# One step count per engine as semaphore, and a planner that charges for tiling changes and second waits

## The reference

```python
x = L0(x, cond, ctx)   # adaln; attention 16 heads x 64 with rotary embedding; gelu
x = L1(x, cond, ctx)   # 16 heads x 8 ("small"); gelu (tanh form)
x = L2(x, cond, ctx)   # 16 heads x 64 without rotation ("flat"); gated gelu
x = L3(x, cond, ctx)   # 16 heads x 8, q and k normalised per head; gates; gated silu
# every attention:
h = ln(x) * (1 + scale) + shift
a = softmax(q(h) @ k(source).T * dh ** -0.5)
x = (a @ v(source)) @ wo + bo + x
```

## Time and profile before

| | us |
|---|---|
| median of 3 runs (lowest, highest) | 1694.85 (1692.47, 1695.61) |
| the profiled execution's own time | 1697.18 |
| its span, first to last instruction | 1695.4 |
| TensorE busy (matmuls) | 1523.6 |
| weight loads | 1202.8 |
| VectorE | 1402.9 |
| ScalarE | 1094.9 |
| GpSimd | 911.8 |

### The profile page before, as it was taken

The page is one execution under the profiler, slowest core; times in us unless marked ns, Lnnn a source line. Parts: engine busy times, 40 slices in busy tenths (PEclk is TensorE's granted clock), DMA queues, the critical chain, the costliest instruction groups (busy, mean ns, idle before and its releaser), DMA issues.

```text
span 1695.4 us, 41504 instructions
## 1 busy us (share of the span) xinstructions
PE 1523.6 (90%) x15228; PEld 1202.8 (71%) x15228; DVE 1402.9 (83%) x3745; ACT 1094.9 (65%) x4765; POOL 911.8 (54%) x1028
## 2 busy tenths in 40 slices
PE   6988999899989899999998989999988999989865
PEld 5876777677768677776777777767766778767643
DVE  5878788988997778898897868998898878888864
ACT  1766778657575777757477667766666686775632
POOL 3746454655664546555665645545565654554432
PEclk9999999999999999999999999999999999999985
DMA  9100000000000000000000000000000000000000
GB/s 325 38 2 1 2 2 2 7 6 3 7 7 2 1 2 2 6 3 7 6 4 7 2 1 2 2 7 2 7 7 7 2 2 1 2 2 3 3 0 4
DMA packets 14441, 20.96 MB, mean 12 GB/s; under 512 B 4064, under 2 KB 10784, under 8 KB 14240
## 3 DMA queue, kind: packets, MB, share of 16 engines
q1 hardware_dynamic: 14240, 18.31, 3.3%
HBM read 17.25 MB, written 1.05 MB: 11 GB/s over the span
## 4 chain that ended last, share of the span: by engine, by line
PE 46%; DVE 36%; POOL 7%; ACT 6%; issue 3%; DMA 0%; SPq 0%; POOLq 0%; DVEq 0%; ACTq 0%
DVE negmax L1025 9%; PE ps L688 9%; PE ps L720 6%; PE ps L571 6%; PE ps L731 5%; ACT E L776 5%; POOL E L879 4%; DVE E L1125 4%; PE ps L703 3%; DVE xn L986 3%; PE ps L651 3%; DVE E L1077 2%; PE ps L665 2%; PE ps L588 2%; PE ps L740 2%
## 5 line engine op out<-in xcount | busy, mean ns | idle before, releaser
L776 ACT ACTIVATE E<-ps,negmax 128x128 f32<-128x128 f32 x2048 | 719.4, 411 | 264.2 <-DVE negmax L1025 263.5
L879 POOL TENSOR_TENSOR E<-E,rinv 128x512 f32<-128x512 f32 x512 | 525.3, 1042 | 382.3 <-DVE rinv L1033 380.6
L776 ACT ACTIVATION_READ_ACCUMULATOR E<-ps,negmax 128x1 f32 x2048 | 512.2, 251 | 0.0
L1025 DVE TENSOR_REDUCE negmax<-ps 128x4 f32<-128x512 f32 x512 | 330.2, 681 | 57.9 <-PE ps L651 33.6
L688 PE MATMUL ps<-consts,E 128*128 128x128 f32 x2048 | 318.9, 287 | 40.0 <-POOL E L879 25.7
L1125 DVE COPY E<-ps 128x512 f32<-128x512 f32 x448 | 300.5, 678 | 59.9 <-PE ps L688 57.6
L688 PEld LDWEIGHTS ps<-consts,E 128*128 128x128 f32 x2048 | 235.6, 146 | 115.6 <-issue 66.7
L872 POOL TENSOR_TENSOR E<-E,prod 128x512 f32<-128x512 f32 x128 | 162.4, 1274 | 74.7 <-DVE prod L1080 74.5
L831 POOL TENSOR_TENSOR rstd<-ve,consts 128x1 f32<-128x1 f32 (+1 forms) x192 | 107.9, 563 | 83.4 <-DVE ve L979 82.9
L720 PE MATMUL ps<-E,VV 128*64 128x128 f32 x2048 | 141.6, 285 | 3.2 <-DVE E L1125 2.6
L785 ACT ACTIVATE VV<-ps 128x512 f32<-128x512 f32 x128 | 77.2, 671 | 90.4 <-PE ps L588 90.3
(11 more groups left out here) (130 smaller groups left out, 2755.3 us busy)
## 6 DMA issues: line engine op xcount, KB each, us to landing
w_f<-res_f SPq DMA_DIRECT2D x6, 256.0 KB, 11.8
qT<-in_x SPq DMA_DIRECT2D x16, 64.0 KB, 1.7
w_wq<-res_wq SPq DMA_DIRECT2D x2, 512.0 KB, 7.8
w_wk<-res_wk SPq DMA_DIRECT2D x2, 512.0 KB, 8.4
w_wv<-res_wv SPq DMA_DIRECT2D x2, 512.0 KB, 9.0
w_wo<-res_wo SPq DMA_DIRECT2D x2, 512.0 KB, 9.8
w_cq<-res_cq SPq DMA_DIRECT2D x2, 512.0 KB, 10.9
w_co<-res_co SPq DMA_DIRECT2D x2, 512.0 KB, 13.8
```

Source lines behind the costliest of these rows:

```text
L776: last = nc.scalar.activation(E[p][:, h, :], bank(u, j * N, (j + 1) * N), ACT.Exp, bias=negmax[p][:, h:h + 1], accum_out=sums[p][:, h:h + 1])
L879: tt(e, e, rinv[p][:, T4 * g:T4 * g + T4].unsqueeze(2).broadcast_to([N, T4, N]), ALU.mult).then_inc(signal["prob"], 1)
L1025: nc.vector.tensor_reduce(negmax[p][:, T4 * g:T4 * g + T4], bank(u).rearrange("p (h m) -> p h m", h=T4), AX, ALU.max, negate=True).then_in ...
```

## The change

Three things change. First, the semaphores: each engine has one, which the last instruction of every step raises by one; a wait is for the step's number in that engine's order. Waits for earlier steps of the same engine are left out by the same rule (`fresh`). Second, on TensorE the wait for banks comes after that for the inputs, and several waits of one kind are sorted with the highest number first. An S step raises once, after its last matmul, instead of once per bank; MX0 to MX2 and PJ0 raise too. Where VectorE needs a result of its own from within a step, it uses `vector_part`. Third, the planner: costs of TensorE's steps without the change of tiling, 0.12 for a step whose tiling differs from the one before, 0.1 for each engine beyond the first that must be waited for, banks chosen with that charge, and rope's VectorE steps held until GpSimd has released the older `prod` tile.

```diff
+RETILE = 0.12
+WAIT = 0.1
-    add(PE, "T", 0.14, (DVE, "norm"), fills=("T",))
+    add(PE, "T", 0.13, (DVE, "norm"), fills=("T",))
...
-            add(PE, "S0", 2.1, ...                      # rope
+            add(PE, "S0", 1.95, ...
-            add(PE, f"S{2 * i}", 1.09, ...              # flat
+            add(PE, f"S{2 * i}", 0.99, ...
-        add(PE, "S0", 1.15, ...                         # small
+        add(PE, "S0", 0.95, ...
-        add(PE, f"PT{g}", 0.46, ...
+        add(PE, f"PT{g}", 0.44, ...
-            add(PE, f"MX{g}", 0.45, ...
+            add(PE, f"MX{g}", 0.24, ...
-        add(PE, f"O{i}", 1.1, ...
+        add(PE, f"O{i}", 0.88, ...
...
+def tiling_of(key):
+    _, step, b, _ = key
+    if step[0] == "S":
+        return "rows of 64" if KIND[b] == "flat" else "rows of 32"
+    return "columns of 32" if step[:2] == "MX" else "columns of 64" if step[0] == "O" else None
+
+def turns_heads(key):
+    return key[0] == DVE and KIND[key[2]] == "rope" and key[1] in ("Q0", "Q1", "K0", "K1")
...
-    vacant = {i: 0.0 for i in range(BANKS)}
+    vacant = {i: (0.0, DVE, 0) for i in range(BANKS)}
...
-            start, banks = max(free[e], known[key]), []
-            if fills[key]:
+            start, banks, extra, met = max(free[e], known[key]), [], 0.0, {}
+            if turns_heads(key) and len(roped) > 1:
+                _, old, old_b, old_s = roped[-2]
+                added = (POOL, "R" + old, old_b, old_s)
+                if added not in end:
+                    continue
+                start = max(start, end[added] + REACH[POOL])
+            if e == PE:
+                for a in after[key]:
+                    if a[0] != PE and number[a] > seen[a[0]]:
+                        met[a[0]] = max(met.get(a[0], 0), number[a])
                 n = len(fills[key])
                 open_ = [i for i in vacant if vacant[i] is not None]
-                if len(open_) < n or fills[key][0] not in OWN and len(open_) - n < SPARE:
+                if n and (len(open_) < n or fills[key][0] not in OWN and len(open_) - n < SPARE):
                     continue
-                banks = sorted(open_, key=lambda i: (vacant[i], i))[:n]
-                start = max(start, vacant[banks[-1]])
-            score = (start, AGE * key[3] - way[key], key)
+                covered = lambda i: vacant[i][2] <= max(seen[vacant[i][1]], met.get(vacant[i][1], 0))
+                banks = sorted(open_, key=lambda i: (max(vacant[i][0], start) + (0 if covered(i) else WAIT), i))[:n]
+                for i in banks:
+                    start = max(start, vacant[i][0])
+                    if not covered(i):
+                        met[vacant[i][1]] = vacant[i][2]
+                extra = WAIT * max(len(met) - 1, 0)
+                if tiling_of(key) != tiling:
+                    extra += RETILE
+            score = (start + extra, AGE * key[3] - way[key], key)
...
+DONE = {_key: _i + 1 for _engine in ORDER for _i, _key in enumerate(ORDER[_engine])}
...
-        bank_full = [sem(f"bank_full{b}") for b in range(BANKS)]
-        bank_drained = [sem(f"bank_drained{b}") for b in range(BANKS)]
+        done = {PE: sem("tensor_done"), DVE: sem("vector_done"), ACTE: sem("scalar_done"), POOL: sem("gpsimd_done")}
+        vector_part = sem("vector_part")
-        signal = {n: sem(n + "_ready") for n in sorted(_total)}
...
-                for unit in units:
-                    if vacant(unit):
-                        if fresh(pe, bank_drained[unit[0]], vacant(unit)):
-                            pe.wait_ge(bank_drained[unit[0]], vacant(unit))
+                def vacated():
+                    for by, count in latest_first(*[EMPTY[n, turn - 1] for n, turn in units if turn]):
+                        if fresh(pe, done[by], count):
+                            pe.wait_ge(done[by], count)
...
                     for r, unit in enumerate(units):
                         q0 = 32 * r
-                        mm(bank(unit), qT[p][q0:q0 + 32, 0, :], kT[p][q0:q0 + 32, 0:T4, :], start=True, stop=True)\
-                            .then_inc(bank_full[unit[0]], 1)
+                        last = mm(bank(unit), qT[p][q0:q0 + 32, 0, :], kT[p][q0:q0 + 32, 0:T4, :], start=True, stop=True)
+                    last.then_inc(done[PE], 1)
...
                 elif step[:2] == "PT":
                     g = int(step[2])
-                    count = AT["prob", f"prob{g}", b, s]
-                    if fresh(pe, signal["prob"], count):
-                        pe.wait_ge(signal["prob"], count)
+                    count = DONE[POOL, f"prob{g}", b, s]
+                    if fresh(pe, done[POOL], count):
+                        pe.wait_ge(done[POOL], count)
+                    vacated()
```

More of the change, by code:

```diff
@@ L218, in schedule @@
     free = {e: 0.0 for e in order}
-    vacant = {i: 0.0 for i in range(BANKS)}
-    end, bank_of, table = {}, {}, "exp"
+    vacant = {i: (0.0, DVE, 0) for i in range(BANKS)}
+    end, number, bank_of, table, tiling = {}, {}, {}, "exp", None
+    seen = {e: 0 for e in order}
     left = {key: len(after[key]) for key in cost}
     ready = [key for key in cost if not left[key]]
-    known = {}
+    known, roped = {}, []
     while ready:
@@ L245, in schedule @@
         table = table_of(key) or table
-        if e == PE and start > free[e] + 0.02:
-            start += REFILL
+        if e == PE:
+            if start > free[e] + 0.02:
+                start += REFILL
+            start += extra
+            seen.update(met)
+            tiling = tiling_of(key)
         end[key] = free[e] = start + cost[key] + (TABLE_LOAD if switch else 0)
         order[e].append(key)
+        number[key] = len(order[e])
         ready.remove(key)
+        if turns_heads(key):
+            roped.append(key)
         for unit, i in zip(fills[key], banks):
@@ L274 @@
         _turns[_bank] += 1
[L275 to L310, removed]
+DONE = {_key: _i + 1 for _engine in ORDER for _i, _key in enumerate(ORDER[_engine])}
+FULL, EMPTY = {}, {}
+for _b, _s, _n in UNIT:
+    _last = {"PV": "MX3", "PJ": "PJ" if KIND[_b] == "small" else "PJ1"}.get(_n)
+    _fill = next(_key for _key in ORDER[PE] if _key[2:] == (_b, _s) and (_key[1] == _last or _n in FILLS[_key] and not _last))
+    FULL[UNIT[_b, _s, _n]] = DONE[_fill]
+for _s in range(S):
+    for _b in range(LAST + 1):
+        for _key, _, _, _, _n in steps_of(_b, _s):
+            if _n:
+                EMPTY[UNIT[_b, _s, _n]] = (_key[0], DONE[_key])
+ROPED = [_key for _key in ORDER[DVE] if turns_heads(_key)]
 ROPE_GROUP = {"Q0": 0, "K0": 1, "Q1": 2, "K1": 3}
@@ L484, in _ @@
                 if step == "sum" and b == L3_CROSS and s + STREAMS < S:
-                    count = AT["sum", "sum", b, s]
-                    if fresh(sp, signal["sum"], count):
-                        sp.wait_ge(signal["sum"], count)
+                    count = DONE[DVE, "sum", b, s]
+                    if fresh(sp, done[DVE], count):
+                        sp.wait_ge(done[DVE], count)
                     load(s + STREAMS)
@@ L624, in step_of @@
                     if b == L3_SELF:
[L625 removed]
+                        mm(bank(u, 0, D), hT[p][:, :], c("spread"), start=True, stop=True).then_inc(done[PE], 1)
                     else:
@@ L1063, in step_of @@
+                    tt(gates[p], bank(u, 0, 3 * D), row("g0", 3), ALU.add).then_inc(done[DVE], 1)
                 elif step in ("Q0", "Q1", "K0", "K1") and k == "rope":
```

561 lines of the change are left out of this document (281 added, 280 removed).

## The result

The change made the kernel slower: 1756.84 us (1752.2 to 1760.1) against 1693.67, ratio 1.0365 with a 95% interval of 1.0349 to 1.0381. The forecast was 1668. The mechanism of rival D is the right one: putting the S steps last cost 76 us in the pair of kernels that differ in it alone, where I had 45, and without that cost the kernel was 15 us faster than before, not 27.

What follows compares the result with a forecast made beforehand. TensorE was taken as the nearest bound (busy 1523.6 of 1695.4 us, 46% of the chain, VectorE 36%). Terms -24 -2 +1 -2 = -27 us gave 1668 from the median 1694.85; range 1630 to 1706.

Steps and rivals of the forecast that it cites:

- rival D: Softmax chains starve as S steps come late by one full-size step, 0.89 us; 45 us lost, 1713 us; chance 0.19.
- the change's first part: Fewer changes of tiling on TensorE: 220 of 891 go, 40 us of its time, -24 us at the end (0 to -73).
- the 30 changes of S: Share of S steps in the 220 fewer tiling changes on TensorE, beside 160 for MX and 30 for O.
- rival C: TensorE's order hardly changes, fewer than 80 tiling changes go: 1690 us; sign: TensorE busy above 1510; chance 0.15.
- D's signs: TensorE busy falls, but L688's counterpart's waits for GpSimd, ScalarE's for maxima and VectorE's for TensorE grow by more.
- The number of changes: Changes of tiling in TensorE's static order: from 891 to about 670.
- Their price: One change of tiling between TensorE's weight loads costs 0.17 to 0.20 us; 0.18 taken.
- What it brings at the end: Share of TensorE's saved time that reaches the end: 0.6, between the chain's 46% and nine tenths.
- The semaphores: Half of about 1000 separate waits on TensorE go: -2 us (0 to -7); the S group's one signal: +1.
- The single signal of an S step: One signal for all banks of an S step: 0 to 0.1 us later each, 160 steps, +1 us (0 to +5).
- the 9 us that I worked out from that page: Saving before the release of the maxima from fewer S signals at 0.026 us each; no term rested on it.
- The gate on rope's products: Planner knows VectorE's rope step waits for GpSimd to release a product tile: -2 us, at most -4.

Runs made afterwards that it cites:

- the pair of kernels that differ in it alone: Changed kernel (1756.84 us) against the same with S steps exempt from the tiling charge in the score (1681.1 us), age price 30.
- S exempt: Changed kernel with the 0.12 us tiling charge left out of the score of S steps alone: 1681.1 us, ratio 0.9911.
- the semaphores alone: Changed kernel with the planner of before, so only semaphores and the order of waits are new: 1690.1 us, ratio 0.9970.
- the three pairs with and without the charges: Changed kernel without score charges against charges on all but S, ages 29, 30, 31: 1704.4 and 1725.8, 1697.0 and 1681.1, 1698.3 and 1676.0 us.
- late S in the old kernel: Kernel before with the gate on rope's product tiles and S steps scored 0.12 us later whatever the tiling: 1809.2 us, ratio 1.0666.
- the changed kernel at ages 29 to 31: Changed kernel with 29, 30 (its own) or 31 as the planner's price of a sequence's age: 1779.5, 1756.8, 1768.8 us.
- S alone: Changed kernel where only S steps bear the tiling charge in the score and no other step bears any charge: 1784.2 us, ratio 1.0518.
- the order alone: Kernel before with the planner of the change but the old semaphores: 1764.1 us, ratio 1.0412.
- the old planner with age 29: Kernel before with the gate on rope's product tiles and age price 29 instead of 30: 1760.4 us, ratio 1.0379.

## Why the prediction was wrong

**The failed step** is in the change's first part: "S steps little, since they need four banks and two spare ones", and the 30 changes of S that I counted as a gain. I treated the score as something that sorts equals. It is a strict first key: while any full-size step can start within 0.12 us, a ready S step isn't taken, however long its way. Ten steps in eleven had their inputs there, which I used as the reason why grouping would work; it is the reason why an S step finds such a rival at nearly every turn. The planners of the kernels, run again, count it: an S step that had its banks and could start no later than the step taken was passed over at 1.1 turns on average before, at 6.1 in the changed kernel and at 1.4 with S exempt. The need for six open banks, on which I had built, hardly moved: it turned an S step away at 3.7, 4.0 and 3.3 turns.

**Rival D was mis-sized.** I let an S step be late by one step, 0.89 us. The traces show 4.6 us more for rope, 3.2 for flat, 4.2 for small: over 32, 64 and 64 steps that is 147 + 205 + 269 = 621 us of added delay, where the prediction had 142. Against the kernel with S exempt it is 693 us, and the loss 76, so 0.11 us of time is lost per us of S delay, where I had 0.32. The two errors work against each other: the delay was taken more than four times too small, the share that reaches the end three times too large, so that 45 came as near to 76 as it did by luck. The chance of 0.19 was too low, and the range, up to 1706, ended below the measured time.

**The signs** that the prediction had named misled. TensorE stayed busy for 1516.4 us, which was the sign for rival C (above 1510). Of D's signs, L709's loads wait 67.6 us for GpSimd where L688's waited 15.7, but such entries also moved by the semaphores alone (67.8 in that run). ScalarE's wait for maxima did not grow, it fell from 263.5 to 216.2; what grew is its whole idle time with a releaser, from 590 to 650 us, by the V banks above all, and so did GpSimd's (770 to 830) and VectorE's (268 to 323).

**The number of changes** was forecast at 670 and is 582; of the 154 runs of tiled steps that went, 106 are MX. **Their price** holds: 0.17 to 0.20 us each by the loads, and in the changed trace the step from L722 to L699 is again 1201.19 - (1200.83 + 0.05) = 0.31 instead of 0.11. **What it brings at the end** failed: 0.6 of 0.18 us was credited per change. TensorE's busy time fell by 27 us in the S exempt kernel for 310 changes against the semaphores alone (0.09 each; the modelled ends hide a part of the price, and the granted clock was 0.963 for 0.970), its waits rose from 162 to 177 us, and the span fell by 11. In the three pairs with and without the charges the gain is between +22 and -21 us. The chain named TensorE at 46%; that share was no pass-through for time taken out at many places that were not the ones it passed.

**The semaphores**: forecast -2 and +1, measured -5.8 by the medians, ratio 0.9970, a little more than forecast. With the old order 600 separate waits are left of 1029, so not quite the half that I expected to go; the change's own 326 come from its order and choice of banks too. The single signal of an S step costs what was estimated: in the kernel before the first maximum starts at the soonest 1.16 us after a small S0's first load and 2.085 after rope's; with one signal 1.21 and 2.135. That is 0.05 us later. Of it, 0.02 is that the fourth strip's last matmul starts after the first strip's (0.556 against 0.536 us after the first load in a small S0, 1.798 against 1.778 in rope's); what the other 0.03 is isn't shown. The Trainium skill ("TensorE: Matmul & The Clock Gate", "The cost: per-tile semaphore tail") gives about 26 ns for each increment and a saving from having only one. Here the reader of the first bank is told later and not earlier, since it had been told before the others; whether some of the 9 us that I worked out from that page came elsewhere, the 5.8 of the whole can't tell.

**The gate on rope's products**: forecast -2, measured nothing (1695.4). By the code it is still needed for other orders (no run shows it): without it nothing in the old planner keeps a rope step of VectorE from standing before the work that leads GpSimd to release its product tile, and the two would block each other. The runs with other scores of the old planner therefore have the gate.

**The clock was missing from the sum.** The mean granted clock is 0.967 before and 0.949 after; between the two levels of 2.4 and 1.2 GHz that is 2 x 0.033 x 1695 = 112 us and 2 x 0.051 x 1755 = 179 us at the lower one. Windows of 300 us, before and after (length, busy and counts of the five engines, then the granted clock):

```profile
400.00:700.00 300.00, 276.45 (x2848) 221.14 (x2847) 251.63 (x671) 203.27 (x860) 168.39 (x191) 0.97 0.01 3
```

```profile
400.00:700.00 300.00, 262.91 (x2629) 219.16 (x2628) 236.88 (x617) 184.22 (x788) 157.62 (x176) 0.92 0.01 3
```

TensorE waits more there and runs at 0.92. In the stretches at the lower level, which last 113 us before and 177 after by the traces, the loads are busy for 74 and 132 us. Loads of a full-size step stand 0.213 us apart there and 0.112 elsewhere, so at full clock the added 58 would be some 30 (an estimate from these rows), and up to 30 of the 63 us could be the slower clock, on top of the waits. By and large the clock goes with the time (0.938 with late S in the old kernel, 0.941 to 0.952 in the changed kernel at ages 29 to 31, S alone and the order alone, 0.951 and 0.956 in S exempt and the old planner with age 29, 0.962 to 0.970 in all at 1705 us and below), but no run holds the clock and changes the waits; this is argued, not shown. Why age 29 costs 65 us in the old planner is open; its plan is 39 us longer too, so more than half of it lies in the order that the planner makes, whatever the chip does with it.

## What to carry to other kernels

A charge for a change of state in a list scheduler's first key is a priority, and it falls on the steps in the costly state: exempt those that feed the other engines (here the scores), or charge the time and not the choice. Compare the planned end before and after first: here the planner's own plan was 59 us longer, and no run was needed to see it. A bubble that is counted right on the bound engine is still not time at the end: ask which steps will be served later for it. And where the order of some thousand steps comes from a greedy planner, measure each edit in pairs over two or three settings of an unrelated constant; here the unrelated constant moved the time by 3.8% in the old planner.

## What the hardware showed that I had not expected

A separate wait on TensorE's queue costs nothing that can be seen in queued work, and the removal of 429 of them, with the single signals of the S steps, brought under 6 us. One signal in place of four, from strips whose matmuls start 0.007 us apart, moves the first reader by 0.05 us to the late side. The granted clock went down with the waits by up to 0.03 in the mean, in a kernel where TensorE is busy 86 to 90% of the time.
